# Cross-attention's out product, residual and normalization on 128-row tiles that cross batches, in a post-norm decoder layer on one core

## The reference, cut to what matters

```python
# x (16, 224, 512), ctx_1024 (16, 750, 512)
x = _layernorm(x + attention(x))                 # 16 heads, causal, out product Wu
q = einsum('bsd,ed->bse', x, Wq) + bq            # cross-attention, one head of 512
k = einsum('btd,ed->bte', ctx, Wk) + bk
v = einsum('btd,ed->bte', ctx, Wv) + bv
attn = softmax(einsum('bse,bte->bst', q, k))
x = _layernorm(x + einsum('bst,bte->bse', attn, v))
x = _layernorm(x + gated_recurrence(x))          # a scan over the 16 batches
```

## Time and profile before

| | us |
|---|---|
| median of 3 runs | 1415.11 (1411.97 to 1417.11) |
| the profiled execution | 1416.02 |
| its span, first to last instruction | 1414.1 |
| granted clock of PE over the span | 0.994 |
| PE busy, share of the span | 98% |
| DVE, ACT and POOL busy, share of the span | 65%, 52%, 40% |

### The profile page before, as it was taken

How to read it: one execution, slowest core, us unless ns; L and a number is a source line. 1 busy time by engine, 2 the same in 40 slices (tenths; PEclk the granted TensorE clock), 3 DMA queues, 4 the chain that set the end, 5 groups by cost and what they waited for, 6 DMA issues and landing times.

```text
span 1414.1 us, 28483 instructions
## 1 busy us (share of the span) xinstructions
PE 1385.4 (98%) x10017; PEld 1211.0 (86%) x10017; DVE 921.9 (65%) x1911; ACT 731.6 (52%) x1989; POOL 569.7 (40%) x475
## 2 busy tenths in 40 slices
PE   7999999999999999999999999999999999999997
PEld 4677777777789999999999988999999999999775
DVE  4589989999657756776677663345453444536697
ACT  4488888888565566656665655222232222222232
POOL 2476767676476565656565620000000000010264
PEclk9999999999999999999999999999999999999999
DMA  7014323335366675667567953010010100000353
GB/s 212 25 56 107 104 75 81 104 104 156 109 172 215 200 240 182 204 195 233 188 205 213 210 155 112 1 27 13 13 26 0 26 13 19 31 1 31 101 186 123
DMA packets 133079, 157.94 MB, mean 112 GB/s; under 512 B 62304, under 2 KB 70496, under 8 KB 133008
## 3 DMA queue, kind: packets, MB, share of 16 engines
q1 hardware_dynamic: 133008, 157.01, 37.8%
HBM read 105.61 MB, written 35.78 MB: 100 GB/s over the span
## 4 chain that ended last, share of the span: by engine, by line
PE 64%; issue 3%; POOL 3%; DMA 1%; DVE 1%; ACT 1%; POOLq 0%; ACTq 0%; DVEq 0%
PE banks L1522 16%; PE banks L1551 11%; PE banks L1007 9%; PE banks L1023 8%; PE banks L1036 6%; PE banks L1553 6%; PE banks L992 5%; POOL o_r L2097 1%; PE banks L977 1%; DMA s_cx_raw<-in_cx 1%; PE banks L1983 1%; PE banks L1053 1%; POOL o_rstd L2105 1%; POOL x_cx_lo L1367 1%; PE banks L2014 0%
## 5 line engine op out<-in xcount | busy, mean ns | idle before, releaser
L461 ACT ACTIVATE s_p<-banks,a_nmax 112x224 f32<-112x224 f32 (+1 forms) x512 | 198.1, 412 | 60.0 <-DVE a_nmax L572 59.9
L759 POOL TENSOR_TENSOR s_p<-s_p,a_rinv 112x896 f32<-112x896 f32 (+1 forms) x128 | 164.5, 1306 | 118.9 <-DVE a_rinv L580 115.8
L1496 POOL CAST m_hi<-w_raw 128x2048 fp32r<-128x2048 f32 x1 | 2.3, 2266 | 407.8 <-PE banks L1522 407.8
L1639 ACT ACTIVATE f_gate<-f_gate 128x448 f32<-128x448 f32 x90 | 52.2, 580 | 198.6 <-DVE f_gate L1762 198.6
L1759 DVE TENSOR_TENSOR f_gate<-banks,f_xg_early 128x448 f32<-128x448 f32 x45 | 28.1, 624 | 189.6 <-PE banks L1553 189.6
L1367 POOL TENSOR_TENSOR x_cx_lo<-s_cx_raw,x_cx_hi 125x512 fp32r<-125x512 f32 x96 | 120.8, 1296 | 37.0 <-ACT x_cx_hi L1136 37.0
L571 DVE TENSOR_REDUCE a_nmax<-banks 112x1 f32<-112x224 f32 x256 | 97.9, 382 | 24.5 <-PE banks L277 23.7
L461 ACT ACTIVATION_READ_ACCUMULATOR s_p<-banks,a_nmax 112x1 f32 x512 | 111.6, 218 | 0.0
L294 PEld LDWEIGHTS banks<-identity,s_p 112*112 112x112 f32 x768 | 88.0, 134 | 21.8 <-issue 2.3
L294 PE MATMUL banks<-identity,s_p 112*112 112x112 f32 x768 | 105.4, 261 | 1.2 <-POOL s_p L759 0.7
L1360 POOL TENSOR_TENSOR s_ct<-s_ct_raw,s_ct 128x750 fp32r<-128x750 f32 x60 | 98.6, 1669 | 0.0
(11 more groups left out here) (255 smaller groups left out, 3727.5 us busy)
## 6 DMA issues: line engine op xcount, KB each, us to landing
s_ct_raw<-in_ct SPq DMA_DIRECT2D x16, 1500.0 KB, 6.7
s_cx_raw<-in_cx SPq DMA_DIRECT2D x16, 1500.0 KB
a_xt<-in_xt SPq DMA_DIRECT2D x16, 448.0 KB, 6.3
a_xrow<-in_x SPq DMA_DIRECT2D x16, 448.0 KB, 5.9
a_xres<-in_x SPq DMA_DIRECT2D x16, 448.0 KB, 6.7
x_scratch<-a_xn SPq DMA_DIRECT2D x16, 448.0 KB, 3.3
x_scratch<-x_xn SPq DMA_DIRECT2D x16, 448.0 KB, 4.6
x_halves<-x_halves SPq DMA_DIRECT2D x16, 448.0 KB, 3.2
```

Of the source, the lines that this page charges most:

```text
L461: e = act.activation((p1 if c else p0)[:, g, h, :], src, ACT.Exp, bias=nmax[:, g % 2, c, h:h + 1], accum_out=rsum[:, g % 2, c, h:h + 1])
L759: pool.tensor_tensor(p[:, g, :, :], p[:, g, :, :], inv, ALU.mult).then_inc(norm_done, 1)
```

## The change

The rows of four batches, 4 x 224 = 896, are taken as 7 tiles of 128. `out(b)` computes the tiles that batch b completes: 1, 2, 2, 2 of them for b mod 4 = 0, 1, 2, 3; rows left over stay in `ot_hi`/`ot_lo`, which get three slots of 128 columns (`PUT` says where a batch's columns go, in two pieces for b mod 4 = 1 and 3). Residual, statistics, normalization and the two stores work on the same tiles. A tile's rows belong to two batches, so 1/sum goes by way of DRAM: `residual_rows` stores `rinv` (224 values), `inverse_rows` loads it by tile. x1's rows for the residual are loaded by tile into `x1b` itself, once `residual` of the batch before has freed it; POOL adds bv in place, now behind `power` and ahead of `cxl`.

The row dots are taken a step ahead from `ahead`, which drops the load L918; `ahead` is refilled only after them. The context is loaded by two DMAs, of 112 and 13 partitions. `x1th(b+1)` moves between the two halves of `exp(b)`. Where the stage begins, ACT and POOL wait for the last residual of self-attention (`r_done`) before their first `cxh`/`cxl`, and only later for its normalized rows (`xn_done`). Loops step by four batches.

```diff
-        x1b = sb("x1b", [R, 2, TC, D])
+        x1b = sb("x1b", [128, TC, D])
...
-        ot_hi = sb("ot_hi", [128, KC, T], F32R)
...
+        ot_hi = sb("ot_hi", [128, KC, 3 * 128], F32R)
...
+        rinv_rows = sb("rinv_rows", [128, 2, TC])
...
+        OF = ((0, 1), (1, 3), (3, 5), (5, 7))
+        SLOT = ((0,), (1, 2), (0, 1), (2, 0))
+        PUT = (((0, T, 0),), ((0, 160, T), (160, T, 0)), ((0, T, 64),), ((0, 96, 288), (96, T, 0)))
+        x1_rows = x1.rearrange("(i q) t d -> i (q t) d", q=4)
...
+        def tiles_of(flat, b):
+            i, q = four(b)
+            return flat[i][128 * OF[q][0]:128 * OF[q][1]].rearrange("(n p) d -> p n d", p=128)
...
+            def inverse_rows(b, at, odd):
+                i, q = four(at)
+                wait(sp, rinv_stored, 16 * (b + 1))
+                with nc.allow_non_contiguous_dma(reason="one value per row"):
+                    sp.dma_start(rinv_rows[:, odd, 0:rows(at)], rinv_dram[i][128 * OF[q][0]:128 * OF[q][1]].rearrange("(n p) -> p n", p=128))\
+                      .then_inc(rinv_in, 16)
+
+            def residual_rows(b, at):
+                wait(sp, rinv_done, b + 1)
+                with nc.allow_non_contiguous_dma(reason="one value per row"):
+                    sp.dma_start(rinv_scratch[b].rearrange("(c p) -> p c", p=R), rinv[:]).then_inc(rinv_stored, 16)
+                wait(sp, r_done, TC * b)
+                sp.dma_start(x1b[:, 0:rows(at), :], tiles_of(x1_rows, at)).then_inc(x1b_in, 16)
...
+            def loads(b, odd, at=None):
+                i, q = four(b if at is None else at)
+                if within(b - 2, B):
+                    inverse_rows(b - 2, (i, q - 2), odd)
...
-                sp.dma_start(cx_raw[:], io["cx"][b].rearrange("(c p) d -> p c d", p=XR)).then_inc(cx_in, 16)
+                shared.load_context(sp, b)
...
                     if within(b + 2, B):
+                        wait(sp, rowbias_done, b + 2)
                         rows_ahead(b + 2)
+                residual_rows(b - 1, (i, q - 1))
...
+            def out(b, at, some=range(TC)):
+                _, q = four(at)
+                n = len(SLOT[q])
...
+                for c in some[0:n]:
+                    slot = slice(128 * SLOT[q][c], 128 * SLOT[q][c] + 128)
                     i = 0
                     for y, w in ((ot_hi, wv_hi), (ot_hi, wv_lo), (ot_lo, wv_hi)):
                         for k in range(KC):
-                            mm = pe.matmul(ps_h[0:R, c, :], y[:, k, c * R:c * R + R], w[:, k, :],
-                                           start=(i == 0), stop=(i == 3 * KC - 1))
+                            mm = pe.matmul(ps_h[:, c, :], y[:, k, slot], w[:, k, :], start=(i == 0), stop=(i == 3 * KC - 1))
                             i += 1
-                    mm.then_inc(out_done, 1)
+                    mm.then_inc(out_done, TC // n)
...
-            def oth(b):
+            def oth(b, at):
+                _, q = four(at)
                 wait(act, out_done, TC * b)
                 for half in range(2):
                     wait(act, ot_done, 2 * b + half + 1)
-                    act.activation(ot_hi[:, 2 * half:2 * half + 2, :], ps_g[:, half, 0:2 * T], ACT.Copy).then_inc(oth_done, 1)
+                    for first, end, place in PUT[q]:
+                        a = act.activation(ot_hi[:, 2 * half:2 * half + 2, place:place + end - first], ot_columns(half, first, end), ACT.Copy)
+                    a.then_inc(oth_done, 1)
...
-            def exp(b):
+            def exp(b, odd):
+                if isinstance(b, int) and b == 0:
+                    act.wait_ge(shared.xn_done, TC * B)
...
                 for c in range(TC):
+                    if c == 1 and within(b + 1, B) and not (isinstance(b, int) and b == 0):
+                        x1th(b + 1)
                     wait(act, max_done, TC * b + c + 1)
...
-            act.wait_ge(shared.xn_done, TC * B)
...
+            act.wait_ge(shared.r_done, TC * B)
...
+                own = isinstance(b, int) and b == 1
+                if own:
+                    dve.wait_ge(x1_in[1], 16)
+                else:
+                    wait(dve, ahead_in, 16 * (b - 1))
                 for c in range(TC):
                     wait(dve, dot_done, TC * b + c)
-                    dve.tensor_tensor_reduce(out=dot[:], in0=x1_raw[odd][:, c, :], in1=kbias[:], scale=1.0, scalar=0.0,
+                    dve.tensor_tensor_reduce(out=dot[:], in0=(x1_raw[1] if own else ahead)[:, c, :], in1=kbias[:], scale=1.0, scalar=0.0,
                                              op0=ALU.mult, op1=ALU.add, accum_out=rowdot[:, c:c + 1]).then_inc(dot_done, 1)
...
-            def residual(b, odd, rows=range(TC)):
+            def residual(b, at, some=range(TC)):
+                i, q = four(at)
+                n = rows(at)
                 wait(dve, x1b_done, b + 1)
...
+                wait(dve, rinv_in, 16 * (b + 1))
+                for c in some[0:n]:
+                    wait(dve, out_done, TC * b + TC // n * (c + 1))
+                    dve.scalar_tensor_tensor(out=r[:, c, :], in0=ps_h[:, c, :], scalar=rinv_rows[:, q % 2, c:c + 1], in1=x1b[:, c, :],
+                                             op0=ALU.mult, op1=ALU.add).then_inc(r_done, TC // n)
...
-                wait(dve, r_done, TC * b)
+                wait(dve, rinv_stored, 16 * b)
...
         def gpsimd(pool):
-            pool.wait_ge(shared.xn_done, TC * B)
...
             pool.wait_ge(shared.bv_in, 16)
 
-            def residual_bias(i, odd):
-                b = 2 * i + odd
-                wait(pool, x1_in[odd], 16 * (i + 1))
-                wait(pool, r_done, TC * (b - 1))
-                pool.tensor_tensor(x1b[:, odd, :, :], x1_raw[odd][:], bv_all[:, :].rearrange("p (a d) -> p a d", a=1).to_broadcast((R, TC, D)),
+            def residual_bias(b, at):
+                n = rows(at)
+                wait(pool, x1b_in, 16 * (b + 1))
+                pool.tensor_tensor(x1b[:, 0:n, :], x1b[:, 0:n, :], bv_all[:, :].rearrange("p (a d) -> p a d", a=1).to_broadcast((128, n, D)),
                                    ALU.add).then_inc(x1b_done, 1)
...
+            def step(i, q):
+                b = 4 * i + q
+                if within(b, B) and not (isinstance(b, int) and b == 0):
+                    ctl(b)
                 if within(b - 2, B):
-                    power(b - 2)
+                    power(b - 2, (i, q - 2))
+                if within(b - 1, B):
+                    residual_bias(b - 1, (i, q - 1))
                 if within(b, B):
                     cxl(b)
+                if isinstance(b, int) and b == 0:
+                    pool.wait_ge(shared.xn_done, TC * B)
...
+            def load_context(sp, b):
+
+                rows = io["cx"][b].rearrange("(c p) d -> p c d", p=XR)
+                for part in (slice(0, R), slice(R, XR)):
+                    sp.dma_start(cx_raw[part], rows[part]).then_inc(shared.cx_in, 16)
```

More of the change, by code:

```diff
@@ L1068, in step @@
                 if isinstance(b, int) and b == B:
[L1069 removed]
+                    out(B - 2, B - 2, range(1, TC))
                 if within(b - 1, B):
@@ L1184, in step @@
                 if within(b - 2, B) and not (isinstance(b, int) and b == B):
-                    separate(act, b - 2)
+                    separate(act, b - 2, (i, q - 2))
                 if within(b, B):
-                    exp(b)
-                if within(b + 1, B) and not (isinstance(b, int) and b == 0):
-                    x1th(b + 1)
+                    exp(b, q % 2)
                 if within(b + 2, B) and not (isinstance(b, int) and b == 0):
@@ L1238, in ztl, with otl @@
                 q.then_inc(ztl_done, 1)
[L1240 removed]
+            def otl(b, at, halves_of=range(2)):
                 for half in halves_of:
                     wait(dve, oth_done, 2 * b + half + 1)
[L1243 removed]
+                    for first, end, place in PUT[four(at)[1]]:
+                        to = slice(place, place + end - first)
+                        low = dve.tensor_tensor(ot_lo[:, 2 * half:2 * half + 2, to], ot_columns(half, first, end),
+                                                ot_hi[:, 2 * half:2 * half + 2, to], ALU.subtract)
                 if half == 1:
[L1245 removed]
+                    low.then_inc(otl_done, 1)
             def row_max(b):
@@ L1266, in statistics @@
+            def statistics(b, at):
+                n = rows(at)
+                each = TC // n
+                for c in range(n):
+                    wait(dve, r_done, TC * b + each * (c + 1))
+                    dve.bn_stats(stats[:, c, :], r[:, c, :]).then_inc(stats_done, each)
+                for c in range(n):
                     dve.wait_ge(pad_done, 1)
-                    wait(dve, stats_done, TC * b + c + 1)
-                    dve.bn_aggr(mv[:, c, :], stats[:, c, :]).then_inc(mv_done, 1)
@@ L1313, in step @@
                 if within(b - 1, B):
```

(4 more changed lines are left out.)

267 lines of the change are left out of this document (134 added, 133 removed).

## The result

The changed kernel takes 1445.36 us (median of 4 runs, 1442.11 to 1446.91) against 1416.11 for the kernel before (4 runs beside it): a ratio of 1.0199, 95% interval 1.0167 to 1.0231. It is slower by 29 us, where the prediction said 1408.0 and left 0.08 for the case that happened. The profiled execution took 1444.24 us, with a span of 1442.5 (before: 1414.1) and a granted clock of 0.984 (0.994).

A forecast was written before the change was run, and what follows sets the result against it. It took PE, running without a gap at 28.5 us per batch, to bound cross-attention. Terms -11.2 - 2.0 + 3.0 + 2.8 + 0.3 = -7.1 us against 1415.1 gave 1408.0 us, range 1402 to 1417.

The forecast's parts named there:

- R: Time from issue to landing of the store of 1/sum in SP's queue: taken as 4.1 us, low end 2.8.
- The fourth rival: SP standing for the store of 1/sum closes a loop; slower from R = 6.3 on, 1430 us at 7.5; chance 0.08.
- The matmuls: Cross-attention on PE: 32 tiles become 28, so 48 matmuls of 0.233 us go, all on the path: -11.2 us.
- The beginning: Cross-attention's start: quicker context load removes PE's waits of 0.94 and 2.07 us; -2.0 us, ends -3.0 and +1.7.
- Lockout at the beginning: Rival: POOL's first cxl holds up self-attention's last normalization on DVE, up to 7.5 us; 1411.7 us in all; chance 0.12.
- x1b late: x1b's later load through POOL and DVE: 0 in a normal batch; rival landing of 5.9 us or more, about 1416; chance 0.17.
- Short steps: Behind batches with b mod 4 = 0, PE is free sooner and waits 1.0 us for exp, three times: +3.0 us.
- The step after a short one: ACT is late for PE, so pth through x1b's load come 1.25 us later; 0.9 us lost three times: +2.8 us.
- The stage's end: PE's wait for ot's low part grows because two-piece copies pay their starts once more: +0.3 us, ends 0 and 0.6.

The follow-up runs named there:

- e5: Changed kernel with the store of 1/sum issued ahead of the 448 KB load of `ahead`, not behind it: 1439.0 us.
- e6: Changed kernel with the store of 1/sum written as 112 packets of 8 bytes instead of 224 of 4, values in another order: 1407.6 us.
- e1: Changed kernel with the store of 1/sum and x1b's load issued ahead of SP's wait for the row dots and the load of `ahead`: 1406.8 us.
- e4: Changed kernel without the store and load of 1/sum by way of DRAM, a constant 1 used instead: 1404.3 us.
- e7: Kernel before, with only the context's load split into two DMAs of 112 and 13 partitions: 1413.1 us.
- e9: Changed kernel with cross-attention's rows taken two by two, so the store of 1/sum has 112 packets of 8 bytes, values in place: 1414.4 us.
- e11: Changed kernel with 1/sum's store and x1b's load earlier, 1/sum's load behind the transposing load, batch 1's row dots later, x1th behind exp again: 1409.5 us.
- e12: Kernel before, plus a store of 224 four-byte values per batch ahead of ct and the transposing load, awaited by nobody: 1493.0 us.

## Why the prediction was wrong

**The failed step** is one term, R, the landing of the store of 1/sum. I took 4.1 us, from a load of 448 KB (4.2) less its head start and 0.3 more, with 2.8 us of a small load as the low end; it measured 8.8. Both are times of other things: the earlier trace rows is a load, and two more loads of that shape in the same stretch took 3.1 and 4.7 us, and the plain loads and stores of the earlier trace rows move rows of 1 or 2 KB. e5 shows that the 448 KB load in front is not what R is made of, e6 that the packets are. The trace of before had no small store to DRAM, so the term was open, and I bounded it by bytes and queueing alone.

**The mechanism was on record; that its formula comes near the time is in part luck.** The fourth rival says that exp ends at 615.1 + R and that ten normal batches and three short ones pay above their slack. At R = 8.8: 10 x (623.9 - 621.09) + 3 x (623.9 - 618.3) = 28.1 + 16.8 = 44.9; less 13.2, plus 0.3, that is +32.0, and 1447 us on 1415.1. Measured 1445.4. Its pieces are off and cancel. The store goes out 8.8 us after the turn (584.54 against 575.75), not 11.3 (603.9 against 592.57), since DVE's first row dot took 0.68 us where I had kept most of the 7.24 of the earlier trace rows: with no x1b in front it now starts just ahead of POOL's ctl (579.57 and 579.60). x1t's transfer took 9.6 us instead of 7.7. And PE waited 26.1 us in place of 44.9, with 13.1 us of slower matmuls behind the waits, which were in no term of mine. It had 0.08 because I gave the long landing one argument, the halves' 11.6 us behind the slow context load, and then took that argument away.

The other steps:

- *The matmuls, -11.2*: right, 5.60 us for 24 and 2.80 for 12.
- *The beginning, -2.0, ends -3.0 and +1.7*: in the changed kernel the second turn came 5.6 us later than before (424.70 against 419.15), as the round trip stands there too. In e1 it came 1.3 us earlier (417.86), in e4 0.6 later (419.77). In all three PE stands some 3.3 us for `x1tl` (row dots of batch 1 ahead of it on DVE, 1.78 and 1.65 us beside POOL's cxl), which I had not listed. In e7 the two waits that I wanted gone went and another of 2.6 us came; its gain lies elsewhere.
- *Lockout at the beginning*: L622, for which I feared up to 7.5 us, started at 381.20 and was held until 382.29, 1.09 us, beside POOL's first cxl; it took 2.60 us in all instead of 1.00. That agrees with the rule of the Trainium skill, "SBUF — State Buffer", section "SBUF: two separate sides", that the shared ports are held for one instruction at a time, by which the prediction expected about 1.3 us.
- *x1b late, 0 in a normal batch*: x1b landed after 9.9 us, beyond the 5.9 that I named, but behind the store; without it 4.5 (e4). With x1b at this place e4 and e6 have every normal batch at 28.5 us.
- *Short steps, +3.0*: at R = 5.0 (e6) only one of the three is late, by 0.3 us; at 5.3 (e9) all are, by 1.1 to 1.9 us. By my sum they pay from R = 3.2 on and 1.8 us each at 5.0; the edge is near 5. The chain of e6's late step, whose turn starts at 618.04, shows which terms were off:

```profile
620.84 0.68 DVE s_dot L1280
...
625.81 4.40 DMA rinv_scratch<-x_rinv
...
631.40 10.21 DMA s_x1t<-x_halves
```

The store goes out 7.8 us after the turn instead of 11.3, and x1t takes 10.2 us instead of 7.7: 3.5 us less and 2.5 more, with R 0.4 below its median.
- *The step after a short one, +2.8*: 0.1 us each, 28.61 us in e4 and e6. It is real only with x1th behind exp (e11, 1.4 each).
- *The stage's end, +0.3*: 1.42 us of waiting against 1.29.

With the trip out of the way the sum of the other terms is -11.2 - 2.0 + 2.8 + 0.3 = -10.1; e4 measured 1404.3 against 1416.0, -11.7, and its span is 10.6 us shorter. In its trace that is -11.2 for the matmuls, +0.6 until the second turn and +0.3 for the steps after a short one: the sum comes near, with two of its terms wrong against each other.

The sentence by the Trainium skill, "DMA: Bandwidth & Descriptors", section "Anatomy of one DMA — SWDGE (gpsimd) path", gave 2 to 2.5 us for R and a sum 3 us lower. That section is on DMAs issued from GpSimd, this store is issued from SP, and the trace gives 8.8 us. By the page's figure the fixed cost would be the smaller part of that.

## What to carry to other kernels

Count a DMA's packets, not only its bytes: here a store of one value per row took as long as a load of 1500 KB, and it delayed the transfers queued behind it whether anyone waited for it or not. When the trace has no row for a new operation, ask which property (direction, packet size, place in the queue) the nearest row doesn't share, let the range reach to where the price would close a loop, and follow that loop once around. Put such a transfer where the queue is idle, lay its values side by side, and reckon, behind a long wait of PE, with slower matmuls after it.

## What was not expected of the hardware

- 224 four-byte writes to DRAM take 8.8 us (7.7 to 12.3 in the other kernels), 112 eight-byte ones 5.0 (to 6.4), a difference of 34 ns per packet from 8.8 to 5.0; loads of 128 or 256 four-byte values landed after 2.1 to 6.0 us (medians of 560 to 680 us).
- 224 such writes per batch that nobody waits for made the kernel before slower by 76 us (e12).
- After waits of PE of 3.3 and 7.65 us its matmuls ran at the lower clock for a while: 1.05 us for four of 224 columns instead of 0.61. The length of the wait alone does not decide: in e1 a wait of 1.53 us was followed by a zt of 7.00 us instead of 5.37 and a granted clock of 0.72 from 418 to 424 us, while in the changed kernel one of 2.36 us was followed by the usual times and a granted clock of 1.00.
- Weights read with a stride of two cost the scores 2% (8.36 against 8.20 us for 48 matmuls); writing a turn's columns with a stride of two cost nothing, 1.30 us for 12.
